# Values of a chunk as two operations, and a new order on all engines

## What is computed

```
x = x + 0.5 * ffn(layernorm(x))          # phase 0
x = x + attention(layernorm(x))          # causal, one head of 128
x = x + 0.5 * ffn(layernorm(x))          # phase 1

ffn: two layers, each
  h = shift_token(x);  q, k, v = split(h @ wqkv)      # 8 heads of 64
  q, k = l2norm and scale, rotary with xpos
  o = softmax(q k over the own window of 64 and the one before, masked) @ v
  x = x + o @ wo
  h = layernorm(shift_token(x)) * g + b
  a, g = split(h @ w1 + b1);  x = x + (a * gelu(g)) @ w2 + b2
```

## Time and profile before

| | us |
|---|---|
| median of three runs | 2849.41 |
| profiled execution, its own time | 2833.46 |
| its span, first to last instruction | 2831.7 |
| PE busy | 2471.9 (87%), 47052 matmuls and as many weight loads |
| DVE busy | 2331.5 (82%) |
| ACT busy | 2073.1 (73%) |
| POOL busy | 1926.8 (68%) |

### The profile page before, as it was taken

How to read it: one execution, slowest core, us unless ns; L and a number is a source line. 1 busy time by engine, 2 the same in 40 slices (tenths; PEclk the granted TensorE clock), 3 DMA queues, 4 the chain that set the end, 5 groups by cost and what they waited for, 6 DMA issues and landing times. The chain is left out here.

```text
span 2831.7 us, 115144 instructions
## 1 busy us (share of the span) xinstructions
PE 2471.9 (87%) x47052; PEld 1887.7 (67%) x47052; DVE 2331.5 (82%) x5957; ACT 2073.1 (73%) x6870; POOL 1926.8 (68%) x2152
## 2 busy tenths in 40 slices
PE   5889988888898898887998888888988899989896
PEld 4666666666666666665997666666666666666664
DVE  7888988887788888884887888888887788888884
ACT  4777877777787778774555777777877777877783
POOL 7878878776677766671105787778877676767672
PEclk8999999999999999998999999999999999999998
DMA  5222222122122222120001122222222122222221
GB/s 136 67 68 65 67 73 61 47 69 69 53 56 64 67 73 68 50 58 16 8 1 40 47 68 64 60 56 68 64 68 60 52 71 72 75 64 58 71 75 30
DMA packets 226250, 170.09 MB, mean 60 GB/s; under 512 B 16146, under 2 KB 190908, under 8 KB 225724
## 3 DMA queue, kind: packets, MB, share of 16 engines
q1 hardware_dynamic: 225724, 162.72, 21.0%
HBM read 91.36 MB, written 71.30 MB: 57 GB/s over the span
## 5 line engine op out<-in xcount | busy, mean ns | idle before, releaser
L3286 POOL TENSOR_TENSOR T<-T,SQ 128x512 f32<-128x512 f32 x512 | 651.1, 1282 | 278.9 <-DVE T L1457 229.3
L2654 ACT ACTIVATE BIGP<-PS,MX 128x96 f32<-128x96 f32 x2048 | 673.0, 371 | 156.6 <-DVE MX L1505 155.6
L3300 POOL TENSOR_TENSOR BIGP<-BIGP,RI 128x384 f32<-128x384 f32 x512 | 418.8, 829 | 255.5 <-DVE RI L1512 255.4
L3294 POOL TENSOR_TENSOR T<-T,RN 128x512 f32<-128x512 f32 x512 | 526.5, 1045 | 21.8 <-DVE RN L1498 21.6
L2654 ACT ACTIVATION_READ_ACCUMULATOR BIGP<-PS,MX 128x1 f32 x2048 | 485.4, 237 | 0.0
L1505 DVE TENSOR_REDUCE MX<-PS 128x8 f32<-128x768 f32 x256 | 243.7, 952 | 209.9 <-PE PS L594 206.8
L559 PE MATMUL PS<-WH,YH 128*128 128x512 f32 x768 | 353.7, 461 | 69.7 <-ACT BIGP L2654 34.9
L2614 ACT ACTIVATE SQ<-PS 128x512 f32<-128x512 f32 x512 | 305.2, 613 | 112.4 <-PE PS L561 78.9
L613 PE MATMUL PS<-PT,VB 32*64 32x96 f32 (+1 forms) x19456 | 272.2, 248 | 110.8 <-issue 104.0
L613 PEld LDWEIGHTS PS<-PT,VB 32*64 32x64 f32 x19456 | 251.8, 133 | 155.0 <-issue 155.0
L1446 DVE TENSOR_REDUCE SS<-SQ 128x8 f32<-128x512 f32 x512 | 335.8, 676 | 19.4 <-ACT SQ L2614 19.3
(11 more groups left out here) (145 smaller groups left out, 5021.8 us busy)
## 6 DMA issues: line engine op xcount, KB each, us to landing
v_rows<-VB SPq DMA_DIRECT2D x256, 256.0 KB, 3.3
VB<-v_rows SPq DMA_DIRECT2D x384, 160.0 KB, 3.3
VB<-v_rows SPq DMA_DIRECT2D x128, 128.0 KB, 2.8
out_dram<-X SPq DMA_DIRECT2D x16, 256.0 KB, 3.8
X<-in_L_attn_x_dram SPq DMA_DIRECT2D x7, 512.0 KB, 4.9
SG<-in_L_ffn_w_dram SPq DMA_DIRECT2D x5, 341.0 KB, 3.6
SG<-in_L_ffn_wqkv_dram SPq DMA_DIRECT2D x4, 384.0 KB, 4.8
SGQ<-in_L_ffn_wqkv_dram SPq DMA_DIRECT2D x4, 256.0 KB, 5.0
```

What stands on the lines that cost most here:

```text
L2654: ins = act.activation(P[:, g, p, 0:KB], PS[:, b, KB * p:KB * p + KB], ACT.Exp, bias=MX[:, m, p:p + 1], accum_out=SM[:, g, p:p + 1])
L3286: pool.tensor_tensor(T1[:, k, :], T1[:, k, :], SQ[:, (2 * n + 1 - x) % 3, :], ALU.add).then_inc(added[x], 1)
L3294: pool.tensor_tensor(heads, heads, RN[:, t % 2, i, 8 * x:8 * x + 8].unsqueeze(2).broadcast_to([128, HEADS, DH]), ALU.mult).then_inc(scaled ...
L3300: pool.tensor_tensor(rows, rows, RI[:, g, :].unsqueeze(2).broadcast_to([128, NB, KB]), ALU.mult).then_inc(p_scaled, 1)
```

## The change

The values of a chunk become two operations, `values(t, 0)` and `values(t, 1)`, of 80 products each by the profile's count (at the start of a sequence 48 and 80), with a signal each. The semaphore `valued` then counts twice as fast. All waits and bank checks of the operation stand in its first half.

```diff
+SPLIT = 3
-        def values(t):
-
-            on.wait_ge(v_moved[t % 2], moved(t))
-            on.wait_ge(p_turned, GPC * (t + 1))
-            for half in range(2):
-                vacant(on, f"O{2 * half}", t)
-                vacant(on, f"O{2 * half + 1}", t)
+        def values(t, part):
+
             begin = 0 if first(t) else -BACK
-            for b in range(begin, BPC):
+            if part == 0:
+                on.wait_ge(v_moved[t % 2], moved(t))
+                on.wait_ge(p_turned, GPC * (t + 1))
+                for k in range(NPAIR):
+                    vacant(on, f"O{k}", t)
+            for b in range(begin, SPLIT) if part == 0 else range(SPLIT, BPC):
...
-            on.wait_ge(valued, t - 1)
+            on.wait_ge(valued, 2 * (t - 1))
...
-            on.wait_ge(valued, t + 1 - PTS)
+            on.wait_ge(valued, 2 * (t + 1 - PTS))
```

More of the change, by code:

```diff
@@ L814, in first_steps @@
-            turn_ln(3)
-            project(2, 0, V)
             turn(1, 0, K)
             turn(1, 0, Q)
-            project(2, 1, V)
[L819 to L827, removed]
+            project(2, 0, Q)
+            turn(1, 1, K)
+            project(2, 1, K)
+            scores(1, 0)
+            project(2, 0, V)
@@ L828, in first_steps @@
+            turn(1, 1, Q)
+            project(2, 1, Q)
+            values(0, 0)
+            values(0, 1)
+            project(2, 1, V)
             project(3, 0, Q)
             scores(1, 1)
+            turn_ln(4)
+            project(3, 0, K)
+            project(3, 1, Q)
+            turn(2, 0, Q)
             turn(2, 0, K)
-            turn(2, 0, Q)
-            project(3, 1, Q)
+            project(3, 1, K)
+            turn(2, 1, Q)
+            project(3, 0, V)
+            project(3, 1, V)
@@ L833, in first_steps @@
+            values(1, 0)
+            values(1, 1)
             turn(2, 1, K)
[L834 to L837, removed]
+            project(4, 0, K)
+            turn_ln(5)
             scores(2, 0)
-            scores(2, 1)
             wo(0)
@@ L844, in local @@
                 t = 2 * s
+                scores(t - 4, 1)
+                turn(t - 3, 0, K)
                 wo(t - 5)
[L846 to L850, removed]
                 turn(t - 3, 0, Q)
-                project(t - 2, 0, V)
                 project(t - 2, 0, Q)
                 scores(t - 3, 0)
-                project(t - 2, 1, V)
-                project(t - 2, 1, K)
-                turn_back(s - 3)
-                turn(t - 3, 1, K)
-                project(t - 2, 1, Q)
-                values(t - 4)
+                turn(t - 3, 1, K)
+                turn_rows(s - 3)
+                project(t - 2, 1, K)
+                project(t - 2, 0, V)
+                values(t - 4, 0)
+                project(t - 2, 1, Q)
+                turn(t - 3, 1, Q)
+                turn_back(s - 3)
+                values(t - 4, 1)
+                project(t - 2, 1, V)
                 to_gate(s - 3, 0)
+                project(t - 1, 0, Q)
+                to_gate(s - 3, 1)
+                scores(t - 3, 1)
                 turn_ln(t)
-                turn(t - 3, 1, Q)
-                to_gate(s - 3, 1)
                 project(t - 1, 0, K)
@@ L938, in attention @@
             to_up(PAIRS - 2, 0)
-            scores(TURN - 1, 1)
             to_up(PAIRS - 2, 1)
@@ L954, in attention @@
             to_up(PAIRS - 1, 2)
-            a_turn_w(0)
-            a_merge(0)
-            a_turn(0, 0)
-            down(PAIRS - 1)
-            a_project(0, 0, Q)
-            turn_y(PAIRS - 1)
             a_scores(0, 0)
@@ L963, in attention @@
             a_scores(0, 1)
+            down(PAIRS - 1)
             a_turn_p(0, 0, 0)
@@ L968, in attention @@
             a_turn_p(0, 1, 0)
+            turn_y(PAIRS - 1)
             a_project(0, 1, Q)
@@ L1262, in attention @@
-            project(TURN + 2, 1, Q)
-            values(TURN)
-            project(TURN + 3, 0, K)
+            project(TURN + 2, 0, Q)
+            turn(TURN + 1, 1, K)
+            project(TURN + 2, 1, K)
+            scores(TURN + 1, 0)
+            project(TURN + 2, 0, V)
+            turn(TURN + 1, 1, Q)
+            values(TURN, 0)
+            project(TURN + 2, 1, Q)
+            values(TURN, 1)
+            project(TURN + 2, 1, V)
             turn_ln(TURN + 4)
-            turn(TURN + 1, 1, Q)
@@ L1277, in attention @@
+            turn_ln(TURN + 5)
+            values(TURN + 1, 0)
+            values(TURN + 1, 1)
+            project(TURN + 4, 0, K)
+            turn(TURN + 2, 1, K)
             scores(TURN + 2, 0)
-            scores(TURN + 2, 1)
             wo(TURN)
         def last_steps():
+            scores(2 * TURN - 4, 1)
+            turn(2 * TURN - 3, 0, K)
             wo(2 * TURN - 5)
-            project(2 * TURN - 2, 0, K)
-            project(2 * TURN - 3, 1, V)
-            turn(2 * TURN - 3, 0, K)
+            turn(2 * TURN - 3, 0, Q)
@@ L1295, in last_steps @@
-            project(2 * TURN - 2, 1, Q)
-            values(2 * TURN - 4)
+            values(2 * TURN - 4, 0)
+            project(2 * TURN - 2, 1, Q)
+            turn(2 * TURN - 3, 1, Q)
+            values(2 * TURN - 4, 1)
+            turn_back(2 * PAIRS - 3)
+            project(2 * TURN - 2, 1, V)
+            project(2 * TURN - 1, 0, Q)
+            scores(2 * TURN - 3, 1)
             to_gate(2 * PAIRS - 3, 0)
-            turn(2 * TURN - 3, 1, Q)
             to_gate(2 * PAIRS - 3, 1)
@@ L1338, in last_steps @@
             turn_y(2 * PAIRS - 2)
-            values(2 * TURN - 1)
-            wo(2 * TURN - 2)
+            values(2 * TURN - 1, 0)
+            values(2 * TURN - 1, 1)
             wo(2 * TURN - 1)
@@ L1777, in first_steps @@
             root(2, 8)
+            turn_p(1, 0)
             root(2, 9)
-            rotate_cos(2, 1, Q)
+            sum_squares(3, 0, Q)
+            y0_up(4)
+            row_max(1, 1)
             sum_squares(3, 0, K)
-            row_max(1, 1)
+            rotate_sin(3, 0, Q)
+            turn_p(1, 1)
+            rotate_cos(3, 0, Q)
             rotate_sin(3, 0, K)
+            row_inverse(1, 1)
             rotate_cos(3, 0, K)
-            sum_squares(3, 0, Q)
-            rotate_cos(3, 0, Q)
-            rotate_sin(3, 0, Q)
-            row_inverse(1, 1)
             turn_p(1, 2)
-            rotate_cos(3, 1, K)
+            sum_squares(3, 1, K)
             turn_p(1, 3)
-            sum_squares(3, 1, K)
             rotate_sin(3, 1, K)
-            row_max(2, 0)
             sum_squares(3, 1, Q)
+            rotate_cos(3, 1, Q)
+            rotate_sin(3, 1, Q)
             root(3, 0)
@@ L1805, in local @@
                 ln_stats(t)
-                row_max(t - 4, 1)
-                ln_stats(t + 1)
-                ln_aggregate(t)
-                root(t - 3, 4)
                 root(t - 3, 5)
-                row_inverse(t - 4, 0)
+                row_max(t - 4, 0)
                 root(t - 3, 6)
                 root(t - 3, 7)
-                ln_aggregate(t + 1)
-                root(t - 3, 8)
-                root(t - 3, 9)
-                y1_low(s - 3)
-                ln_eps(t)
-                y1_high(s - 3)
-                turn_p(t - 4, 0)
-                y0_up(t - 1)
+                root(t - 3, 8)
+                ln_aggregate(t)
+                root(t - 3, 9)
+                sum_squares(t - 2, 0, K)
+                y0_up(t - 1)
+                rotate_sin(t - 2, 0, K)
+                row_max(t - 4, 1)
+                row_inverse(t - 4, 0)
+                rotate_cos(t - 2, 0, K)
+                ln_stats(t + 1)
+                turn_p(t - 4, 0)
+                y1_low(s - 3)
+                turn_p(t - 4, 1)
+                y1_high(s - 3)
+                ln_aggregate(t + 1)
+                row_max(t - 3, 0)
                 rows_stats(s - 3)
@@ L1853, in local @@
                 root(t - 2, 7)
-                turn_p(t - 3, 1)
-                root(t - 2, 8)
-                root(t - 2, 9)
-                rotate_cos(t - 2, 1, Q)
-                gate(s - 3, 0)
-                row_max(t - 3, 1)
-                sum_squares(t - 1, 0, K)
-                gate(s - 3, 1)
+                root(t - 2, 8)
+                turn_p(t - 3, 0)
+                root(t - 2, 9)
+                row_max(t - 3, 1)
+                sum_squares(t - 1, 0, Q)
+                sum_squares(t - 1, 0, K)
@@ L1891, in attention @@
             root(TURN - 3, 7)
             root(TURN - 3, 8)
+            sum_squares(TURN - 2, 0, K)
             root(TURN - 3, 9)
+            rotate_sin(TURN - 2, 0, K)
             a_stats(0, 0)
+            row_max(TURN - 4, 1)
+            row_inverse(TURN - 4, 0)
             y1_low(PAIRS - 3)
+            rotate_cos(TURN - 2, 0, K)
+            turn_p(TURN - 4, 0)
             y1_high(PAIRS - 3)
-            turn_p(TURN - 4, 0)
+            turn_p(TURN - 4, 1)
+            row_max(TURN - 3, 0)
@@ L1965, in attention @@
             root(TURN - 1, 9)
+            row_max(TURN - 2, 1)
```

(77 more changed lines are left out.)

1028 lines of the change are left out of this document (499 added, 529 removed), and 112 rows, old and new, of tables (FIRST_USERS, LAST_USERS, ROTA).

## The result

The changed kernel takes 2770.63 us in the median (2769.33 to 2777.3, four runs) against 2845.28 for the kernel before: ratio 0.974, 95% interval 0.971 to 0.977, 75 us less. The forecast was 2822 with 27 us less. The profiled execution has a span of 2768.4 us against 2831.7, 63.3 us less.

What follows compares the result with a forecast made beforehand. PE is busiest but pauses as dense small products outrun instruction loading. Pauses -1.6, waits +1.6, clock -0.4 make -0.4 us a round, x 58 = -23, and -4 once: -27 us, median 2822; own range 2775 to 2865, overall 2745 to 2890.

Steps and rivals of the forecast that it cites:

- The pauses: PE's issue stops in values and scores, 2.28 us a round: splitting and moving give -1.6, bounds -2.28 and 0.
- The count by boundary positions: Estimate of pauses from where 254-instruction block boundaries fall in values and scores: 2.9 us a round old, 0.6 to 0.7 new.
- The new wait in front of `values(t-4,0)`: PE waits for DVE's transpose behind rows_stats and reciprocal: 2.3 us in every round, bounds 1.9 and 4.
- The waits together: PE's waits per round: +2.3 new, -0.2 others, about half a microsecond taken in short idle gaps, so +1.6 us.
- waits other than the new one: Before the first W1 product, scores(t-3,0) and values(t-3,0): 1.1 us a round against 1.55, -0.2, bounds -1.3 and +1.5.
- PE's work stays: On PE: no product is added or removed, so only code density and who waits for whom change.
- the clock: PE's clock falls to 1.2 GHz after pauses; fewer pauses give -0.4 us a round, bounds -1.2 and +0.5.
- Outside the two windows: First and last steps, entry to attention: reordered entry pulls weight turns up, 0 to -5 us once, -4 taken.
- More gain: Rival: the waits shrink with the pauses, -1.7 us a round, -99 us, 2750; chance 0.22.
- The longer wait: Rival: wait before values(t-4,0) is longer, deciding from 2.7 us; at 4.0 the time is 2924; chance 0.17.
- of another kind: Rival: the pauses are not a matter of density and stay, +1.4 us a round, +81, 2930; chance 0.05.
- the clock falls in each round: Rival: the new wait makes PE's clock fall 58 times, +0.5 us a round, 2874; chance 0.14.
- The signs: Forecast wrong if the wait before values is under 1.5 or over 3, or issue time stays above 50.

Runs made afterwards that it cites:

- experiment 1: Changed kernel with both pairs of values halves put next to each other again in the steady rounds: 2888.39 us, ratio 1.013 to the kernel before.
- experiment 2: Changed kernel with only the second pair, values(t-3,0) and values(t-3,1), next to each other: 2814.13 us, ratio 0.986 to the kernel before.
- 10: Kernel before with the values halves parted, values(t-4,0) ahead of project(t-2,1,Q), turn_y between the halves of values(t-3): 2925.04 us, ratio 1.026.
- 12: Kernel before with wo(t-4) between the two scores of t-2 in place of behind them: 2861.21 us, ratio 1.006.
- 3: Changed kernel with row_inverse(t-4,1) moved on DVE ahead of row_max(t-3,0): 2742.17 us, ratio 0.962 to the kernel before.
- 4: Changed kernel with row_inverse(t-4,1) moved behind rows_aggregate and ln_eps: 2801.26 us, ratio 0.985 to the kernel before.
- 6: Changed kernel with row_inverse(t-4,1) ahead of row_max(t-3,0), V projection ahead of K's on PE, copy_v ahead of square on ACT: 2728.11 us, ratio 0.957.
- 11: Kernel before with only the second pair of values halves parted, by turn_y; first pair adjacent in its old place: 2848.43 us, ratio 1.001.

## Why the prediction was too small

The order of its steps is kept. All sizes are per round of the first window.

- *The pauses*: -1.6 expected, -(63.7 - 3.9)/28 = **-2.14** measured, near the bound of -2.28, so this term was too small by 0.54. That density makes them is shown in both directions: experiments 1 and 2 bring 0.77 and 0.37 us back, 10 and 12 take 0.57 and 0.34 away. The count by boundary positions overstated what remains: 0.7 expected, 0.14 found. What a pause ends with can be read as well, since the trace has the times of the 374 fetches of the earlier trace rows. After 2370 in the kernel before, two of them land at 2373.06 and 2376.68, and the products of the earlier trace rows resume 1.37 and 1.48 us later; of the 88 pauses over half a microsecond in `values` and `scores`, 86 end 1.20 to 1.62 us after a landing, a stretch that takes up some 5% of the time. The 3.73 us of the earlier trace rows are one pair and not the best: thirteen pairs of resumptions one block apart in the first phase lie 3.41 to 4.25 us apart.
- *The new wait in front of `values(t-4,0)`*: 2.3 expected, 61.6/28 = **2.2** measured, on the instruction and by the chain that were named; 4.16 us from `turn_rows` to the values for 4.2. Experiments 3, 4 and 6 move it as the loop says.
- *The waits together*: +1.6 expected, **+0.79** measured, and this is the step that failed most. All idle time but issue was (124.8 - 63.7)/28 = 2.18 before and (1080.40 - 993.35 - 3.9)/28 = 2.97 after. The forecast started from the 1.55 us of one good round instead of the 2.18 of the mean, and put 1.1 on waits other than the new one where 0.77 came. In its own terms it took 0.2 and half a microsecond off the other idle time, where 2.18 - 0.77 = 1.41 went, more than its bound of 1.3. The two waits on ACT, 0.87 a round in the earlier trace rows, are down to scraps and one on DVE of 9.1/28 = 0.33; neither `copy_q` nor the second pair's values holds PE by as much as the hand count gave them.
- *"PE's work stays"*, with -0.4 from the clock: PE's busy time **rose by 0.45**, (993.35 - 980.83)/28. The mean clock of the first phase is 0.98 for 0.97 and that of the second unchanged, so the clock gave little between these two executions. Two partings a round account for the rise: 0.25 us each from start to start (2 x 1.12 for 1.99), 0.3 to 0.4 each in the rounds at the full clock that stand with experiment 2. No bound of the forecast had it.
- *Sum*: -2.14 + 0.79 + 0.45 = -0.90, against -0.4; over 58 rounds -52 for -23. Pauses and waits were off by 1.35 the one way, work and clock by 0.85 the other, so the sum came nearer than its terms did. Outside the two windows: -12 for -4, most of it in the part between the phases.
- *The rivals.* "More gain" (2750) had the pauses right and came nearest in its sum, 2770.63 lying between it and the forecast and below the forecast's own 2775, with the price of the new wait as forecast. The longer wait did not come. The pauses went, so they were not of another kind. That the clock falls in each round is out: the mean is 0.963 for 0.960 over the run.
- *The signs.* Those that were to show the forecast wrong (a wait under 1.5 or over 3, issue time above 50) did not come up. They tested the mechanism, which held, and not the sizes of the waits and of PE's work.

A part of the 75 us isn't in the traces: the profiled executions are 63 us apart, since that of the kernel before was 12 us faster than its median. That part may be the clock: it was 0.960 in that execution and 0.953 to 0.958 in the seven that stood beside experiment 1, against 0.960 to 0.965 in the four of the changed kernel.

Two expectations on what belongs together, those of experiments 10 and 12, failed as well. Parting the values is worth 43 us for the second pair in the new order (experiment 2), nothing in the old (11), and costs 82 where the first half then meets the loop through DVE (10). So the gain was found with neither edit alone, as far as these runs go (experiment 1 also moves `turn_back` later): the split removes pauses of PE, and only an order whose other waits don't close in on the freed time keeps the gain. Which of the many swaps between the old and the new order does that was not taken apart.

## What to carry to other kernels

Where an engine stops in the middle of a run of small instructions and the profile names no releaser, count the instructions between two resumptions and look when the instruction queue's fetches land: an engine can outrun its own code, and parting dense pieces with long operations removes the pauses. Then look for the longest loop that leaves this engine and comes back between two of its operations; here one reciprocal queued behind statistics it has nothing to do with cost 28 us. The bank behind it set the next limit; freeing that one moved the wait and left PE's idle time as it was. Take the mean of many rounds as the base of a sum of waits, not the best round, and count every switch between small and large products as work.

## What the hardware showed unexpectedly

Instruction loading bounds PE in this kernel at about 254 instructions in 3.4 to 4.2 us (thirteen pairs of resumptions; no two fetches after 150 us start less than 3.27 us apart); spread out, it cost 3.9 us in 28 rounds, against 63.7. The Trainium skill, "Runtime: NRT & Kernel Launch", section "Instruction fetch mechanics", calls it hidden; in this kernel it was nearly hidden only after the change. A run of 160 small products in two pieces costs 0.25 us more than in one (medians 1.12 twice for 1.99), although nothing waits between them.
